# The visits of the attention spread anew over the gaps of the dense runs, every fourth one sharing a gap with the visit ahead of it

## The reference

```
x = x + 0.5 * ffn(layernorm(x))      # softmax router over 32 experts, top 8, kept below 0.8 of the sum
x = x + attn(layernorm(x))           # 16 heads of 16, 4 heads of keys and values, rope, softmax, Wo
x = x + 0.5 * ffn(layernorm(x))
# ffn: for each expert  h = silu(x Wg) * (x Wu);  out += (h Wd) * weight[token, expert]
# attn, per batch and head: softmax(q k^T * scaling) v, over 1024 x 1024 scores
```

## Time and profile before

| what | us |
|---|---|
| median of three runs | 2270.76 (2270.74 to 2271.02) |
| the profiled execution | 2270.94 |
| its span | 2269.1 |
| PE busy | 2200.3 (97%) |
| DVE busy | 1626.9 (72%) |
| ACT busy | 1166.9 (51%) |
| POOL busy | 1072.5 (47%) |

### The profile page before, as it was taken

How to read it: one execution, slowest core, us unless ns; L and a number is a source line. 1 busy time by engine, 2 the same in 40 slices (tenths; PEclk the granted TensorE clock), 3 DMA queues, 4 the chain that set the end, 5 groups by cost and what they waited for, 6 DMA issues and landing times.

```text
span 2269.1 us, 47149 instructions
## 1 busy us (share of the span) xinstructions
PE 2200.3 (97%) x18794; PEld 1487.7 (66%) x18794; DVE 1626.9 (72%) x3203; ACT 1166.9 (51%) x1885; POOL 1072.5 (47%) x908
## 2 busy tenths in 40 slices
PE   3999999999999999999999999999999999999998
PEld 2888875556565565565566566566655665688887
DVE  7756678887887877787877877777777754454543
ACT  4433331666556556565556565566656556433332
POOL 1767654444444444444434443434344334466655
PEclk9999999999999999999999999999999999999999
DMA  5211121011111120110211111010110110101010
GB/s 222 80 41 37 39 58 31 23 42 31 35 31 43 33 51 25 34 37 24 53 41 32 31 36 32 20 42 16 26 47 6 29 32 20 30 26 40 22 40 20
DMA packets 157956, 88.50 MB, mean 39 GB/s; under 512 B 103588, under 2 KB 149924, under 8 KB 156968
## 3 DMA queue, kind: packets, MB, share of 16 engines
q1 hardware_dynamic: 157592, 85.45, 14.1%
q10 hardware_dynamic: 144, 0.03, 0.0%
HBM read 63.14 MB, written 11.80 MB: 33 GB/s over the span
## 4 chain that ended last, share of the span: by engine, by line
PE 89%; DVE 7%; DMA 1%; issue 1%; ACT 1%; POOL 1%; SPq 0%; POOLq 0%; DVEq 0%
PE PS L1211 43%; PE PS L1229 21%; PE PS L1241 11%; PE PS L1274 10%; DVE arena L960 2%; PE PS L1193 1%; PE PS L1303 1%; DMA X<-wd 1%; PE PS L1253 1%; DVE arena L937 1%; DVE arena L945 1%; PE PS L1179 0%; DVE turned L923 0%; DVE turned L925 0%; DVE arena L922 0%
## 5 line engine op out<-in xcount | busy, mean ns | idle before, releaser
L1211 PE MATMUL PS<-XT,WGU 128*128 128x256 f16 x9216 | 1112.0, 273 | 14.2 <-DVE turned L925 8.8
L1211 PEld LDWEIGHTS PS<-XT,WGU 128*128 128x128 f16 x9216 | 875.9, 98 | 236.9 <-issue 129.9
L606 POOL TENSOR_TENSOR arena<-arena 128x512 f16<-128x512 f32 x384 | 451.2, 1175 | 1065.9 <-ACT arena L675 1065.9
L960 DVE TENSOR_REDUCE arena<-PS 128x1 f32<-128x512 f32 x1024 | 656.5, 684 | 269.3 <-PE PS L1241 265.4
L691 ACT ACTIVATE arena<-PS,fac 128x512 f32<-128x512 f32 x1024 | 647.4, 685 | 270.7 <-PE PS L1253 270.5
L668 ACT ACTIVATE arena<-PS,fac 128x512 f32<-128x512 f32 x384 | 264.4, 689 | 771.7 <-PE PS L1211 771.7
L1229 PE MATMUL PS<-WD,arena 128*128 128x256 f16 x4608 | 568.3, 273 | 2.6 <-POOL arena L606 2.4
L601 POOL TENSOR_TENSOR arena<-arena 128x512 f32<-128x512 f32 x384 | 501.7, 1306 | 85.9 <-DMA arena<-ce_scratch 44.5
L1229 PEld LDWEIGHTS PS<-WD,arena 128*128 128x128 f16 x4608 | 430.4, 98 | 145.6 <-issue 94.6
L937 DVE SCALAR_TENSOR_TENSOR arena<-arena,PS 128x512 f32<-128x512 f32 x384 | 261.2, 680 | 247.4 <-ACT arena L668 246.6
L1241 PE MATMUL PS<-arena 48*128 48x512 f16 x1024 | 318.9, 382 | 14.9 <-DVE arena L960 12.8
(11 more groups left out here) (117 smaller groups left out, 729.5 us busy)
## 6 DMA issues: line engine op xcount, KB each, us to landing
arena<-ce_scratch SPq DMA_DIRECT2D x256, 128.0 KB, 3.2
arena<-wgu SPq DMA_DIRECT2D x4, 1536.0 KB, 13.4
arena<-q_scratch SPq DMA_DIRECT2D x192, 32.0 KB
arena<-ktab_c SPq DMA_DIRECT2D x16, 256.0 KB, 4.0
q_scratch<-arena SPq DMA_DIRECT2D x32, 128.0 KB, 1.8
out<-X SPq DMA_DIRECT2D x8, 512.0 KB, 3.0
X<-wd SPq DMA_DIRECT2D x2, 1536.0 KB, 24.0
X<-x SPq DMA_DIRECT2D x1, 3072.0 KB, 12.1
```

Source lines behind the costliest of these rows:

```text
L606: pool.tensor_tensor(hs[1][:, d % HS, :], tw[d % 2], hs[0][:, d % HS, :], ALU.subtract).then_inc(lo_done, 1)
L960: dve.tensor_reduce(mx[:, half * REP * QT + c:half * REP * QT + c + 1], PS[:, B_MAX + half, :], AX_X, ALU.max).then_inc(max_taken, 1)
L1211: ins = pe.matmul(PS[:, b, j * HALF_G:(j + 1) * HALF_G], WGU[w][:, kt, part * CHUNKS + c + j, :], XT[r][:, k % 2, kt, half * HALF_G:(half ...
```

## The change

`visit_table` gives groups of visits now. The forty visits ahead of the first still have one gap each. From visit 0 on, visit v goes to gap `(v - (v % 4 == 1)) * 15 // 11`, counted over all three positions alike: visits with v % 4 == 1 go to the gap of the visit ahead of them, and the others follow at one or two gaps (two or three behind a shared one). There are still 11 visits to 5 slots, and the last are in slot 310, as before. In a shared gap PE runs S of v - 1, then V, then S of v. The loops over a position go over its group; on ACT and DVE the second visit of a shared position 0 stands behind `high(d)` and `gated(d + 1)`. Of shared gaps that have values, 36 are at position 0, 46 at position 1 and 46 at position 2 (the last has values alone), which leaves 127 with scores on both sides. Position 0 is empty in 127 of slots 79 to 310; before, it was always filled there. Some output projections move by a slot or two.

```diff
@@ -75,20 +75,23 @@
 FIRST = 2 * PER_GROUP + 16
 
 
+
 def visit_table():
 
-    at, v, d = {}, -AHEAD, FIRST
-    while v < VISITS + 2:
-        for pos in range(3 if v < 0 or (d - FIRST) % 5 == 4 else 2):
-            if v < VISITS + 2:
-                at[d, pos] = v
-                v += 1
-        d += 1
+    at, gap = {}, 3 * FIRST
+    for v in range(-AHEAD, 0):
+        at[divmod(gap, 3)] = (v,)
+        gap += 1
+    for v in range(VISITS + 2):
+        where = divmod(gap + (v - (v % 4 == 1)) * 15 // 11, 3)
+        at[where] = at.get(where, ()) + (v,)
     return at
 
 
 VISIT = visit_table()
-SLOT_OF = {v: d for (d, pos), v in VISIT.items()}
+SLOT_OF = {v: d for (d, pos), group in VISIT.items() for v in group}
 
 
 def head_of(fill):
...
@@ -734,10 +737,12 @@
                 k, s = divmod(d, PER_GROUP)
                 if d + 1 < SLOTS:
                     gate(d + 1)
-                if (d, 0) in VISIT:
-                    visit(VISIT[d, 0])
+                for v in VISIT.get((d, 0), ())[:1]:
+                    visit(v)
                 if 0 <= d < SLOTS:
                     high(d)
+                for v in VISIT.get((d, 0), ())[1:]:
+                    visit(v)
                 if d in D_HIGH_AT:
                     d_high(D_HIGH_AT.index(d) + 1)
                 if d == 1 or d == 3:
...
@@ -1096,13 +1102,15 @@
                 k, s = divmod(d, PER_GROUP)
                 if d % PER_HALF == 1 and d > 1:
                     add_dense(d // PER_HALF - 1)
-                if (d, 0) in VISIT:
-                    visit(VISIT[d, 0])
+                for v in VISIT.get((d, 0), ())[:1]:
+                    visit(v)
                 if d + 1 < SLOTS:
                     gated(d + 1)
+                for v in VISIT.get((d, 0), ())[1:]:
+                    visit(v)
+                if d + 1 < SLOTS:
                     product(d + 1)
-                if (d, 0) in VISIT:
-                    unit_ends(VISIT[d, 0])
+                unit_ends(VISIT.get((d, 0), ()))
                 if s - 1 in join_slots(k):
                     rope_sum(k - 1, join_slots(k).index(s - 1))
                 if d == -1 or d == 0:
...
@@ -1365,18 +1371,18 @@
             for d in range(-1, SLOTS + 1):
                 if d + 1 < SLOTS:
                     gate_or_up(d + 1, 0)
-                if (d, 0) in VISIT:
-                    visit(VISIT[d, 0])
+                for v in VISIT.get((d, 0), ()):
+                    visit(v)
                 if d + 1 < SLOTS:
                     gate_or_up(d + 1, 1)
-                if (d, 1) in VISIT:
-                    visit(VISIT[d, 1])
+                for v in VISIT.get((d, 1), ()):
+                    visit(v)
                 if len(EVENTS[d]) > 1:
                     event(d, 1)
                 if 0 <= d - 1 < SLOTS:
                     down(d - 1)
-                if (d, 2) in VISIT:
-                    visit(VISIT[d, 2])
+                for v in VISIT.get((d, 2), ()):
+                    visit(v)
                 if EVENTS[d]:
                     event(d, 0)
 
```

More of the change, by code:

```diff
@@ L982, in visit, with unit_ends @@
                         turn_outputs(q // QT)
[L985 to L989, removed]
+            def unit_ends(visits):
+                for v in visits:
+                    f = v + AHEAD
+                    if f < VISITS and f % FILLS == FILLS - 1:
+                        max_rows(f // FILLS)
             def turn_outputs(hv):
@@ L1124, in _ @@
                 if (d, 2) in VISIT:
-                    unit_ends(VISIT[d, 1])
-                    visit(VISIT[d, 2])
+                    unit_ends(VISIT.get((d, 1), ()))
+                    for v in VISIT[d, 2]:
+                        visit(v)
                 if d in OUT_AT:
@@ L1148, in _ @@
                     event(d, 0)
[L1149 to L1152, removed]
+                unit_ends(VISIT[d, 2] if (d, 2) in VISIT else VISIT.get((d, 1), ()))
         @block.tensor
```

## The result

The changed kernel takes 2303.2 us, median of four runs (2302.02 to 2305.43), against 2270.76: a ratio of 1.0144, with a 95% interval of 1.0128 to 1.016. That is 32 us slower. I had forecast 2267, with slower at 0.17 and a range up to 2277.

The account below looks back on a forecast made before the run. PE was taken to bound the kernel. Profiled execution 2270.94 - 11.4 + 10.6 - 3.7 + 0.7 = 2267.1, so 2267.0 us for the median; the range for 8 in 10 was 2256 to 2277.

Parts of the forecast that it names:

- Fewer changes of arrangement: On PE, in 127 shared gaps: eight changes instead of nine per four visits, 0.09 us saved a gap, -11.4 us.
- rival C: On PE in shared gaps: values behind scores need no change, 127 x 0.09 more saved, 2256 us; chance 0.07.
- Joins: U behind a join waits for DVE with less cover where position 0 is empty: +10.6 us.
- the pair at nothing: Second scores of a shared gap find their banks read in time, as values cover both readers: no cost.
- E: Pair waits at position 1, 46 gaps by 0.22 us, 2277; or removed change never on PE's path, 2271; chance 0.07.
- DVE's backlog elsewhere: PE's other waits for DVE, away from joins, fall as positions 0 and 1 are both filled less often: -3.7 us.
- rival D: DVE falls behind where a visit at position 2 is followed by one at position 0: 2279 us; chance 0.14.

Follow-up runs that it names:

- e4: The changed kernel with the next group of visits moved to position 0 behind the 12 of 18 joins where it was empty; 2294.0 us.
- e3: The kernel before, its spacing kept, with visit v - 1 moved into the gap of visit v (v % 4 == 1); 2278.4 us.
- e9: e3 with 19 pairs kept apart: sixteen whose second scores had waited and three that uncover a join; 2253.4 us.
- e11: e3 with 19 other pairs kept apart, chosen among those that did not wait; 2281.7 us.
- e1: The kernel before with the new spacing but no shared gaps, each visit in a gap of its own; 2297.7 us.
- e10: The changed kernel with POOL's L586 run over 128 of its 1024 columns; 2296.9 us.

## Why the prediction was wrong

**Right.** PE's own row and its waits account for the whole difference. Fewer changes of arrangement: -11.4 forecast, -11.9 measured; scores to values costs like the changes that it replaces, so rival C (the load hidden) falls. Joins: +10.6 forecast, +11.3 measured, and e4 shows that the lost cover is its cause.

**Wrong, the pair at nothing.** I worked out that V gives the readers 2.40 us and that they need 1.55 to 2.05 "as long as neither reader comes late", and then priced the lateness at zero. It is +20.6, the largest term. Before, S of v starts one S, one dense run and V after S of v - 1: 0.54 + 1.41 + 1.86 = 3.8 us. Sharing takes 1.4 us off that, at the very place where the maxima of the first S must be read in between. DVE's other work (a router piece of 2 us, `normalise`, `max_rows`, `gated` and `product` at position 1) fits into 3.8 with 1.28 of maxima and doesn't fit into 2.4. e3, e9 and e11 show this without the spacing: in e3's trace sixteen pairs of 127 carry nearly all of it, and each of them has such a lump ahead in DVE's list (for one, at slot 181, the reading of a join). It was a rival of mine (E), but with 0.22 us at 46 gaps, where it is 0.4 to 4.5 us at nine.

**Wrong, DVE's backlog elsewhere.** I forecast -3.7, since positions 0 and 1 are filled together less often. It is +11.1. e1 shows it with no shared gap: rest 43.3 for 26.8, up to 5.1 of it by the clock (10.2 us at 0.50). The mean load of DVE is the same; what counts is that a fixed lump has a long enough gap behind it. Before, the 3.3 us from position 1 to the next position 0 stood just where the lumps stand in DVE's list, in four slots of five. The new spacing puts visits anywhere in its cycle of 20 slots against lumps in a cycle of 24, so the lumps meet short gaps. Slot 116 of e1 shows one such place; that this is all of it was not tested. It was rival D in kind, which I gave 0.14 and 12 us, but not in place: D's visit, at position 1 behind filled positions 2 and 0, loses over 0.4 us three times in the changed kernel, 2.5 together. The largest losses of e1 are at position 2.

Of the +11.1, some 3.6 are the clock, of which the forecast has nothing. Behind two of the four waits of PE of over 2 us the granted clock was 0.50, at slots 117 and 204; behind the other two, at slots 188 (2.07) and 277 (2.22), it stayed at 1.00:

```profile
core 0: us, PE busy (x), PEclk, DMA share, GB/s
688.00:690.00 2.00, 2.00 (x10) 0.50 0.02 2
...
1184.00:1186.00 2.00, 2.00 (x21) 1.00 0.04 12
...
1299.00:1301.00 2.00, 1.70 (x7) 0.50 0.08 8
1301.00:1303.00 2.00, 2.00 (x12) 0.50 0.02 5
...
1789.00:1791.00 2.00, 2.00 (x20) 1.00 0.23 61
```

```profile
688.79 2.60 PE L1235 MATMUL PS<-WD,arena 128*128 128x256 f16 x12
691.24 1.47 PE L1217 MATMUL PS<-XT,WGU 128*128 128x256 f16 x12
```

Behind the wait of slot 117 (2.02 in the list) the twelve matmuls of W take 2.45 us (688.79 to 691.24) and not 1.32: 1.13 lost, with the granted clock at 0.50, which is 1.2 of 2.4 GHz. Behind the 4.4 us wait of slot 204, W and the join lose 1.22 and 1.27. In e10 the wait of slot 188, again 2.07, was followed by 0.50, and in e3 one of 3.13 was not. So the same wait costs more in one execution than in another, and part of the difference between executions of these kernels (2302.0 to 2305.4 for the changed one) can be this. In the kernel before PE never waits over 1.2 us in this stretch, and the clock stays at 1.00.

**What stays open.** No run takes the router's or the layernorm's pieces out, so the rest column is read from traces alone. What decides whether the clock falls behind a wait of PE is not shown.

## What to carry to other kernels

Moving work of a full engine nearer together saves its changeovers only where the engine that reads its results has nothing else in its list there; so work out the readers' slack at each place with what stands in their list at that place, not at a clean one. A mean load of 76% says nothing about this. Where a table sets the order, exceptions from a trace (19 of 127 pairs) turned 8 us slower into 17 us faster, and the control with 19 others shows that it must be these.

## What the runs showed of the hardware

- Going from row-tiled scores to column-tiled values costs 0.09 us on PE (0.31 from the last start of S, where two pairs are 0.22 apart), as going from dense runs to scores does. That it is a weight load that nothing hides is a reading of its size.
- An elementwise maximum of two 128x32 tiles in SBUF took DVE 0.15 us alone, and 4.10 us across three operations of POOL that followed one another; 2.02 with the last of them shortened. Elsewhere it ended with the first of two such operations (0.60 us at 986.48).
- Where the clock fell behind a wait of PE, it halved: behind 2.0 us the next W took 2.45 for 1.32 us, behind 4.4 us W and the join took 2.53 for 1.31 and 2.56 for 1.29. That is 0.5 to 0.6 of the wait once more. Behind two waits of 2.1 and 2.2 us in the same execution it did not fall.
